# Capping the row gathers of a mixture-of-experts combine at three in flight, with one semaphore per expert choice

## What is computed

```
xf = layernorm(x1).reshape(S, C)                     # S = 4096 tokens, C = 512
shared_out = silu(xf @ shared_gate.T) * (xf @ shared_up.T) @ shared_down.T   # hidden size 1024
topk_idx, w, _ = _route(xf, router_w, correction_bias)                  # 4 of 16 experts per token
combine = zeros((S, E)).at[arange(S)[:, None], topk_idx].add(w)
hw = silu(g) * u * combine.T[:, :, None]             # g, u: each expert's gate and up, hidden size 128
routed = einsum('esh,ehc->sc', hw, down_w)
return x1 + shared_out + routed
```

## Time and profile before

| | |
|---|---|
| median of 3 runs | 1027.45 us (1026.65 to 1032.85) |
| span of the profiled execution | 1028.5 us |
| time of that execution around its span | not shown by the page |
| TensorE, VectorE, GpSimd busy over the span | 996.0, 660.2, 435.6 us |
| last stage (803 to 1029 us): TensorE, VectorE, GpSimd busy | 200.56, 130.91, 133.03 us |
| gathers L2114 in the last stage | 128, 133.0 us busy |
| data moved by gathers in the last stage | 33.56 MB of 51.28 MB |

### The profile page before, as it was taken

How to read it: one execution, slowest core, us unless ns; L and a number is a source line. 1 busy time by engine, 2 the same in 40 slices (tenths; PEclk the granted TensorE clock), 3 DMA queues, 4 the chain that set the end, 5 groups by cost and what they waited for, 6 DMA issues and landing times.

```text
span 1028.5 us, 21007 instructions
## 1 busy us (share of the span) xinstructions
PE 996.0 (97%) x6750; PEld 601.8 (59%) x6750; DVE 660.2 (64%) x1534; ACT 380.4 (37%) x776; POOL 435.6 (42%) x508
## 2 busy tenths in 40 slices
PE   8999999999999999999999999999999978999988
PEld 7775644444444454457777777787777533334433
DVE  5968698873688889775555555555455345655856
ACT  3646444332643433314444444444444211111111
POOL 0816321211243222155454554554452457557652
PEclk9999999999999999999999999999999989899999
DMA  9736868679353515029999999998887659778565
GB/s 347 265 111 215 286 185 231 203 225 253 117 172 134 143 62 155 30 72 256 259 268 263 262 265 245 269 259 242 242 250 216 184 181 305 225 270 291 172 202 185
DMA packets 176635, 219.02 MB, mean 213 GB/s; under 512 B 101224, under 2 KB 112360, under 8 KB 175528
## 3 DMA queue, kind: packets, MB, share of 16 engines
q1 hardware_dynamic: 152792, 139.05, 46.3%
q0 software_dynamic: 23760, 78.79, 25.1%
HBM read 124.72 MB, written 70.27 MB: 190 GB/s over the span
## 4 chain that ended last, share of the span: by engine, by line
PE 84%; DVE 6%; issue 4%; DMA 2%; another core or an unknown queue 1%; ACT 1%; POOL 0%; SPq 0%; DVEq 0%; ACTq 0%
PE bank L1073 18%; PE bank L947 18%; PE bank L1136 12%; PE bank L963 9%; PE bank L1097 9%; PE bank L1148 5%; PE bank L1056 5%; PE bank L1087 2%; PE bank L722 1%; DMA arena<-in_x 1%; PE bank L799 1%; DVE arena L1575 1%; PE bank L979 1%; DMA arena<-pt_dram 1%
## 5 line engine op out<-in xcount | busy, mean ns | idle before, releaser
L947 PE MATMUL bank<-arena 128*128 128x512 f16 x960 | 218.3, 379 | 1.2 <-DMA arena<-pt_dram 1.0
L1073 PE MATMUL bank<-arena 128*128 x1716 | 211.1, 273 | 0.9 <-DVE arena L1614 0.9
L1073 PEld LDWEIGHTS bank<-arena 128*128 128x128 f16 x1716 | 163.0, 98 | 26.4 <-issue 1.4
L2114 POOL DMA_INDIRECT arena<-y_dram,arena x128 | 133.0, 1039 | 89.9 <-issue 38.4
L2069 POOL DMA_INDIRECT arena<-xr_dram,arena x143 | 141.0, 986 | 58.2 <-issue 46.4
L947 PEld LDWEIGHTS bank<-arena 128*128 128x128 f16 x960 | 94.2, 99 | 109.6 <-DMA arena<-pt_dram 1.4
L1136 PE MATMUL bank<-arena 128*128 128x512 f16 x576 | 138.5, 391 | 18.3 <-issue 17.7
L1097 PE MATMUL bank<-arena 128*128 x429 | 115.4, 378 | 0.5 <-ACT arena L1407 0.5
L1344 ACT ACTIVATE arena<-arena 128x512 f16<-128x512 f32 x64 | 40.3, 629 | 202.6 <-DVE arena L1622 100.8
L1136 PEld LDWEIGHTS bank<-arena 128*128 128x128 f16 x576 | 56.6, 100 | 95.3 <-issue 33.9
L1889 DVE SCALAR_TENSOR_TENSOR arena<-bank,arena 128x128 f32<-128x128 f32 x143 | 41.7, 292 | 108.7 <-ACT arena L1396 84.9
(11 more groups left out here) (226 smaller groups left out, 1332.9 us busy)
## 6 DMA issues: line engine op xcount, KB each, us to landing
y_dram<-arena SPq DMA_DIRECT2D x143, 256.0 KB
arena<-in_x SPq DMA_DIRECT2D x8, 1024.0 KB, 12.3
xr_dram<-arena SPq DMA_DIRECT2D x16, 512.0 KB, 3.9
x_dram<-arena SPq DMA_DIRECT2D x8, 1024.0 KB, 5.5
arena<-in_gu_w SPq DMA_DIRECT2D x16, 512.0 KB, 3.6
out<-arena SPq DMA_DIRECT2D x32, 256.0 KB
arena<-x_dram SPq DMA_DIRECT2D x5, 1024.0 KB
arena<-x1s_dram SPq DMA_DIRECT2D x20, 256.0 KB
```

What stands on the lines that cost most here:

```text
L947: last = mm(bank[half][:, :], (gu_hi_s, gu_lo_s)[wp][:, c, at:at + H], xt[:, xv * KC + kc, :], start=(n == 0), stop=(n == 3 * KC - 1))
L1073: last = mm(gate_up_bank(s, s)[:, 0:2 * H], rows[:, xv * KC + kc, :], only((gu_hi_r, gu_lo_r)[wp], e, slice(kc * 2 * H, (kc + 1) * 2 * H)) ...
L2114: pool.indirect_dma_start(out=ybuf[n % RING][:, e, :], out_offset=None, in_=y_dram[:, :], in_offset=bass.IndirectOffsetOnAxis(ap=row_of[:, ...
```

## The change

Semaphores now belong to the choice and not to the slot of the ring: the gathers of choice e of all 32 turns count on `s_ye_in[e]`. VectorE waits, ahead of every addition, for the one gather it adds. Since each semaphore counts a sequence of gathers, GpSimd keeps them apart: with IN_FLIGHT = 3, it issues gather i only when gather i - 3 has landed. The ring's wait stays. Number, size and order of gathers and additions stay, as does everything on the other engines; lines behind the first edits shift, so that L1952, L1960, L1965, L1975 and L2114 of before are L1949, L1957, L1962, L1972 and L2117.

```diff
+IN_FLIGHT = 3
...
-        s_yg = [sem(f"y_gathered{r}") for r in range(RING)]
...
-        s_ylast = [sem(f"last_y_gathered{e}") for e in range(TOP_E)]
+        s_ye_in = [sem(f"y_gathered_of_choice{e}") for e in range(TOP_E)]
...
                 n, e = p // TOP_E, p % TOP_E
                 k, m = turns[n]
-                if n == len(turns) - 1:
-                    dve.wait_ge(s_ylast[e], 16)
-                elif e == 0:
-                    dve.wait_ge(s_yg[n % RING], 16 * TOP_E * (n // RING + 1))
+                dve.wait_ge(s_ye_in[e], 16 * (n + 1))
...
+            def landed(i):
+
+                pool.wait_ge(s_ye_in[i % TOP_E], 16 * (i // TOP_E + 1))
+
             for n, (k, m) in enumerate(turns):
                 if n >= RING:
                     pool.wait_ge(s_cmb, TOP_E * (n - RING + 1))
                 for e in range(TOP_E):
+                    if n * TOP_E + e >= IN_FLIGHT:
+                        landed(n * TOP_E + e - IN_FLIGHT)
                     pool.indirect_dma_start(
                         out=ybuf[n % RING][:, e, :], out_offset=None, in_=y_dram[:, :],
                         in_offset=bass.IndirectOffsetOnAxis(ap=row_of[:, e * T + m:e * T + m + 1], axis=0)
-                    ).then_inc(s_ylast[e] if n == len(turns) - 1 else s_yg[n % RING], 16)
+                    ).then_inc(s_ye_in[e], 16)
```

## The result

| | before | changed |
|---|---|---|
| median of 4 runs, same chip | 1030.15 us (1026.65 to 1036.98) | 1044.07 us (1040.85 to 1046.08) |
| ratio | 1 | 1.0133, 95% interval 1.0074 to 1.0191 |
| span of the profiled execution | 1028.5 us | 1039.0 us |
| time of the profiled execution itself | not shown | 1040.85 us |

The change makes the kernel slower by 1.3%, where I had forecast 2% faster. On a later machine it was worse: 4.85% slower. What follows explains both, and the second number is nearer to what the change costs where nothing else disturbs the kernel. Medians are over all executions, while the ratios leave out those over 1.5% above the fastest of their kernel, so a ratio is not quite the quotient of two medians; two of the twelve executions of e18, at 2095.64 and 3677.16 us, are among those left out, and what happened in them is not known.

The account below looks back on a forecast made before the run. The prediction took TensorE as the bound, with 33.4 us lost in the last stage: 1028.5 - 33.4 (stretches) + 11.7 (gather supply behind TensorE's floor) = 1006.8 us of span, forecast as 1006 us, range 994 to 1043.

Parts of the forecast that it names:

- What bounds the kernel now: Whole kernel: TensorE is the bound, busy 97%; the last stage loses 33.4 us on it, so the floor is 995.1 us.
- disturbed stretches: Spans of the last stage, such as 826 to 839 us, where TensorE idles and its clock falls; 33.4 us lost.
- Step (5): Last stage: the stretches where TensorE idles mostly go with the change, giving back 33.4 us.
- "remote" waits: VectorE's last-stage waits whose releaser the profile cannot explain: 58.8 us in 5 waits, forecast to fall under 15 us.
- Rival A: Last stage: the cap changes nothing that matters and the stretches stay; 1028 us, range 1018 to 1036, chance 0.28.
- Step (1): GpSimd's gathers: three in flight give 1.37 us per gather in quiet, 1.83 us at most in loaded stretches.
- The 1.38: Pace in us assumed for the 98 gathers outside loaded stretches, beside 30 at 1.83; mean 1.49.
- Step (2): End of the last stage: first gather at 807.7, plus 127 x pace, plus 9.7 us; 1006.8 us at pace 1.49.
- Step (3): VectorE's additions: waiting for one gather instead of four gives nothing by itself; its 0.5 us per chunk is hidden by TensorE.
- Step (4): GpSimd's ring wait stays, with one more wait on the same instruction: put at nothing, at most 3 us.
- Rival B: Last stage: gather supply becomes the bound, slower above 1.60 us per gather; 1043 us, chance 0.19.
- What to look for: Signs in the changed profile; against the supply sum: gather waits at L1949 over some 20 us, TensorE waiting behind them.

Follow-up runs that it names:

- e18: The changed kernel with four gathers in flight instead of three, timed on a disturbed machine (chip 10): 1024.56 us, ratio 0.993 to the kernel before.
- e7: The changed kernel with six gathers in flight and six semaphores in turn, on an undisturbed machine: 1002.75 us, ratio 1.0103 to the kernel before.
- e5: The kernel before, unchanged, profiled again on an undisturbed machine: 1001.27 us, span 999.5 us.
- e13: The changed kernel again, unaltered, on a disturbed machine (chip 14): 1044.43 us, ratio 1.0113 to the kernel before.
- e10: The changed kernel with SyncE's tile loads and stores cut to 16 of 512 columns, on a disturbed machine: span 1022.6 us.
- e1: The changed kernel with four gathers in flight instead of three, on an undisturbed machine: 1017.56 us, ratio 1.0156 to the kernel before.
- e4: The kernel before, uncapped, with a one-column copy on GpSimd ahead of each gather to pace it, on an undisturbed machine: 1028.74 us, ratio 1.0276.
- e6: The changed kernel again, unaltered, on an undisturbed machine: 1042.39 us, ratio 1.0485 to the kernel before.
- e8: The changed kernel with two gathers in flight instead of three: span 1100.2 us.
- e14: The kernel before, uncapped, with gathers paced by a small GpSimd copy ahead of each, on a disturbed machine (chip 14): 1025.5 us.
- e17: The kernel before, uncapped, with gathers paced by a small GpSimd copy ahead of each, timed on disturbed chip 10: 1029.68 us, ratio 1.0009.
- e11: The changed kernel with six gathers in flight, on a disturbed machine (chip 2): 1035.88 us, ratio 1.0033 to the kernel before.
- e2: The changed kernel with eight gathers in flight and eight semaphores in turn, VectorE's single waits kept, on an undisturbed machine: 997.75 us, ratio 0.9996.
- e3: The changed kernel, cap of three kept, but VectorE waits for all four gathers of a turn at once: 1040.93 us, ratio 1.0394 to the kernel before.
- e9: The changed kernel with each VectorE addition cut to 8 of 512 columns: span 1051.9 us.

## Why the prediction was wrong

- **What bounds the kernel now** was read rightly for the first machine: 33.4 us in the disturbed stretches, floor 995.1 us. The floor was then seen: e7's span is 993.4, e5's 999.5. What I could not know from one trace is that the stretches are there on some machines, or at some times, only.
- **Step (5), the stretches go with the change,** was right in its effect on the two disturbed machines where it ran: "remote" waits of VectorE from 58.8 us to none, and none in e13. The reason I leaned to, the depth of six gathers, is not borne out: e10 has "remote" waits with three in flight. Rival A's own evidence, that the first stretch had under three in flight, was the better reading; its conclusion that the time stays fell, because the cap slows the pace, and the fastest run of gathers is what goes with the waits. What the Trainium skill says (SBUF — State Buffer, Who interferes with whom), that DMA never contends with a compute engine, is not refuted by these runs, since no cause was found; but on the disturbed machines the late results were absent where gathers were slower.
- **Step (1), the pace under the cap, is the step that failed.** I worked it out as (3.8 + 0.3) / 3 = 1.37 us in quiet and took 1.83 for a quarter of the gathers, 1.49 on average. It measured 1.754. The 3.8 us came from a median over the few gathers whose landing the view could place. The changed kernel's chain shows 5.75 us from issue to landing, and in each cycle one wait for a landing and one step of GpSimd advance four gathers in 7.68 us. I had the 1.83 in hand as an upper bound for loaded stretches, and nearly the whole stage was like that: with 30 gathers at 1.83, a mean of 1.754 puts the other 98 at 1.73 and not at 1.38. The 1.38 is the term that was mis-sized, and it makes nearly all of the 32 us between the forecast and the measured span.
- **Step (2), from pace to end,** was right to 1 us: 1038.5 against 1039.0, and so in the ten profiled runs of capped or paced kernels e1 to e4, e6 to e8, e13, e14 and this one, from 993 to 1100 us (e17 is 2 us off). It does not hold where TensorE and not the last gather sets the end: e11's last issue + 9.7 is 1016.7 and its span 1029.3. Put 1.754 in the place of 1.49 and the forecast is 1040.
- **Step (3)** was right in that single waits cost nothing (e2, 0.9996). That they are "what keeps the cap from costing more" did not show: e3, without them, took 1040.93 us, no longer than the changed kernel elsewhere. **Step (4)** as well: e2 has the double waits on GpSimd and is at 0.9996.
- **Rival B is what happened:** place, mechanism and price, with a point of decision of 1.60 us (on an undisturbed machine, where the kernel before ends near 998, the same sum puts it at 1.42). I gave it 0.19 because a quiet stretch ran at 1.40 us per gather; at the 5.4 to 5.75 us to landing of the changed kernel's chain, that rate means about four in flight, an estimate, so it was no evidence for a queue capped at three.
- **What to look for** was right on both counts that I named for (2) being wrong: the waits at L1949 are 82.4 us, far over 20, and TensorE waits behind them.

## What to carry to other kernels

A cap on transfers in flight sets their pace at the round trip divided by the cap. Take the round trip from issue to landing in the loaded stage, from the chain or from several landings, and compare the pace with what the consumer needs before anything else. Here three in flight meant 1.75 us against the 1.46 that TensorE's pace asks for.

If the consumer's last item sets the end, the end is first issue + count x pace + a fixed tail, and this simple sum was better than any picture of waits: sharpening the waits of the consumer (one gather instead of four) moved nothing.

Before explaining a hole in a trace, see whether it is there on another machine, and before ordering runs by a mean, see whether the effect is part of that mean. A change that removes a disturbance of some machines has to be priced on the others.

## What the runs showed of the hardware

- The same kernel has medians of 995 to 1037 us on six machines. On the slower four, VectorE and ScalarE wait up to 17.2 us for TensorE's results in the last stage, in profiles whose fastest 16 gathers in a row are 1.28 to 1.39 us apart, and TensorE's own starts are held back in the same stretches; on the other two machines they are not. Where the fastest 16 are 1.48 us apart or more, no such wait of VectorE was seen on any machine (e9, e13, e14, e17 and the changed kernel on disturbed ones). What happens in these stretches was not found; SyncE's tile traffic is not needed for them (e10). That they come from other use of the machine is possible and wasn't tested.
- Gathers of 256 KB land later the more of them are in flight. Pace times in flight, an upper estimate of the round trip, is 4.5 us with two, 5.2 with three and 6.2 with four, with SyncE's traffic beside it, and 4.6 with three and most of that traffic gone.
- GpSimd's gather instruction takes 0.95 us with VectorE idle and up to 1.34 beside an addition of VectorE. The Trainium skill (SBUF — State Buffer, Who interferes with whom) says that a VectorE instruction with two inputs in SBUF contends with GpSimd's reads; the mean falls from 1098 to 990 ns when the additions shrink (e9), which agrees. It did not matter for the pace.
